# Decoder kernel: decay exponents from running gate sums brought in by DMA, some norm steps on GpSimd, two reorderings on TensorE, and dummy products in the tail

## The reference, cut to what matters

```python
q = l2norm(silu(h @ Wq)); k = l2norm(silu(h @ Wk)); v = silu(h @ Wv)
beta = sigmoid(h @ Wb)
g = -exp(A_log) * softplus(h @ Wa + dt_bias)
alpha = exp(g)
def step(S, (q_t, k_t, v_t, a_t, b_t)):
    S = S * a_t
    delta = (v_t - k_t @ S) * b_t
    S = S + outer(k_t, delta)
    return S, (q_t @ S) * scale
o = rms_norm(scan(step)) * o_norm_w * silu(h @ Wg)
x = x + o @ Wo
m = rms_norm(x)
y = x + square(relu(m @ W_fc)) @ W_proj
x = layernorm(x0 + y)            # then cross attention, layernorm, experts, layernorm
```

## Time and profile before

| | before |
|---|---|
| median of 3 runs | 709.38 us (707.37 to 709.8) |
| profiled execution, its own time | 709.69 us |
| its span, first to last instruction | 707.7 us |
| busy in the span: PE / DVE / ACT / POOL | 614.6 / 476.1 / 407.2 / 276.4 us |
| weight loads on PE | 507.6 us |
| mean granted clock of TensorE | 0.917 |

### The profile page before, as it was taken

One profiled execution on the slowest core, in us unless ns is written; L12 is line 12 of the kernel. 1 busy time (PEld: TensorE's weight loads), 2 busy tenths in 40 slices (PEclk: granted clock), 3 DMA queues, 4 the chain that ended last, 5 costly groups with the idle time before them and its releaser, 6 DMA issues.

```text
span 707.7 us, 14886 instructions
## 1 busy us (share of the span) xinstructions
PE 614.6 (87%) x5453; PEld 507.6 (72%) x5453; DVE 476.1 (67%) x1841; ACT 407.2 (58%) x723; POOL 276.4 (39%) x233
## 2 busy tenths in 40 slices
PE   2889999999998999999988999999899986339940
PEld 1456887888888778888787888887888875227740
DVE  4747944787888568888895787679657864513315
ACT  2734537898755587876646878756154653114413
POOL 3446002444444125426421443474212252226763
PEclk9999969999998999999999999999589997559985
DMA  8403130002105100020050002001401430032243
GB/s 253 154 1 75 46 70 1 2 1 46 31 1 115 17 1 15 2 49 24 21 128 3 1 16 46 16 20 48 81 1 44 161 87 10 13 72 27 24 93 107
DMA packets 78383, 34.02 MB, mean 48 GB/s; under 512 B 49968, under 2 KB 73849, under 8 KB 78184
## 3 DMA queue, kind: packets, MB, share of 16 engines
q1 hardware_dynamic: 74344, 30.89, 17.2%
q0 software_dynamic: 3968, 2.20, 2.3%
HBM read 20.04 MB, written 14.40 MB: 49 GB/s over the span
## 4 chain that ended last, share of the span: by engine, by line
PE 63%; DVE 18%; issue 6%; ACT 5%; DMA 4%; POOL 3%; SPq 1%; ACTq 0%; POOLq 0%; DVEq 0%
PE ps L681 21%; PE ps L646 6%; PE ps L722 4%; DVE prod L1868 4%; DVE blk_t L1875 4%; PE ps L834 3%; PE ps L1255 3%; PE ps L745 3%; PE ps L1245 3%; PE ps L822 3%; PE ps L1051 2%; PE ps L920 2%; PE ps L930 1%; POOL slots L595 1%; PE ps L941 1%
## 5 line engine op out<-in xcount | busy, mean ns | idle before, releaser
L490 POOL TENSOR_TENSOR att<-att,br 128x512 f32<-128x512 f32 x32 | 33.3, 1043 | 179.1 <-ACT att L1318 179.1
L471 POOL TENSOR_TENSOR of<-oss,mhalf 128x4 f32<-128x4 f32 x32 | 32.7, 1021 | 86.8 <-DVE oss L1762 86.2
L471 POOL TENSOR_TENSOR st<-st,mhalf 128x4 f32<-128x4 f32 (+1 forms) x23 | 22.4, 973 | 100.8 <-DVE st L1988 67.1
L1868 DVE TENSOR_TENSOR prod<-kn,blk_t 128x126 f32<-128x126 f32 (+35 forms) x244 | 53.0, 256 | 1.1 <-DMA kn<-n_blocks 1.1
L1875 DVE TENSOR_TENSOR blk_t<-blk_t,prod 128x126 f32<-128x126 f32 (+35 forms) x244 | 51.3, 249 | 0.1
L1264 ACT ACTIVATE uo<-ps 128x512 f32<-128x512 f32 x56 | 33.6, 600 | 20.0 <-PE ps L681 19.8
L1264 ACT ACTIVATE ogT<-ps 128x512 f32<-128x512 f32 x32 | 19.1, 596 | 42.9 <-PE ps L646 42.7
L681 PEld LDWEIGHTS ps<-kT 128*128 128x128 f32 x256 | 32.7, 192 | 14.9 <-issue 14.5
L681 PE MATMUL ps<-qT,kT 128*128 128x128 f32 x256 | 42.9, 324 | 0.4 <-DVE att L1767 0.4
L941 PEld LDWEIGHTS ps<-ones,kT 128*128 128x128 f32 x256 | 32.6, 192 | 11.5 <-issue 10.7
L1725 DVE SCALAR_TENSOR_TENSOR uo<-uo,of,gate_sb 128x128 f32<-128x128 f32 x128 | 38.6, 363 | 3.1 <-POOL of L471 3.1
(11 more groups left out here) (249 smaller groups left out, 1764.6 us busy)
## 6 DMA issues: line engine op xcount, KB each, us to landing
tt_blocks<-gate_sb SPq DMA_DIRECT2D x4, 512.0 KB, 3.0
TT<-tt_blocks SPq DMA_DIRECT2D x16, 128.0 KB, 2.6
Nm<-in_L_ffn_w SPq DMA_DIRECT2D x1, 2048.0 KB, 9.1
kn<-in_L_ffn_w SPq DMA_DIRECT2D x8, 256.0 KB, 4.5
n_blocks<-Nm SPq DMA_DIRECT2D x16, 96.0 KB, 2.6
kn<-n_blocks SPq DMA_DIRECT2D x4, 384.0 KB, 3.4
t_blocks<-blk_t SPq DMA_DIRECT2D x4, 384.0 KB, 2.3
slots<-qT SPq DMA_DIRECT2D x5, 274.0 KB, 3.9
```

The costliest lines, as they stand in the source:

```text
L471: pool.tensor_tensor(out_ap, in_ap, mhalf[:, 0:n], ALU.pow).then_inc(done, 1)
L490: pool.tensor_tensor(heads(att[:, slot(kb, m)]), heads(att[:, slot(kb, m)]), bc(br[:, kb % 2, unit(m)].unsqueeze(2), [P, HG, P]), ALU.mult ...
L1868: counts.append(st.step(tt(pr, bc(bn_[:, j, i0:i0 + n].unsqueeze(2), [P, n, ncol]), bc(blk_t[:, j, 0:ncol].unsqueeze(1), [P, n, ncol]), AL ...
```

## The change

Decay. `head_eg` now splits g into a part on a coarse grid and a rest, and beside the three sums of before it makes a fourth and one product that gives the running sums as 32 rows of 128. ACT copies the negated sums as columns (`neg_sums`) and the rows (`sum_rows`). SP stores the rows to memory and loads them back, spread over all partitions, one load of 128 by 512 for each unit (two large ones of 128 by 2048 for batch 0). POOL adds the -30000 above the diagonal (`decay_mask`), and ACT takes exp with the column as bias, one instruction for each of the four heads (for batch 0 DVE subtracts the column and masks in `first_exponents`, and ACT takes exp in one instruction). PE's `decay` is gone. `head_eg` is moved into the middle of `between`, ahead of `q_proj` 4, and `v_proj` 4 waits until ACT has read the bank.

Banks. The key projections of batches 1 to 3 go to `EB` in place of `KS`, and the key grams of batch 0 alternate between two banks.

GpSimd. The scaling of the rows of h (`head_h`), two norm steps of four instructions each (`post_a`, `post_x2`) and the clearing of `blk_t` go from DVE to POOL. The final half-products keep theirs on DVE.

Order. `gate_out` stands ahead of the post pieces on DVE. `qk_gram` 3 and 4 stand ahead of `post_y`. `post_aT` stands after the transpose of the first key unit in `levels`. ACT makes its last copy of level 4 before the next silu.

Dummy products. `keep_busy(n)` issues n products of 128 by 512 in bf16 whose result nobody reads, at eight places of the tail and 32 ahead of the experts.

```diff
-            def decay_cols(kb, m):
-                pool.wait_ge(sm["gate_step"], kb * GATE_OPS + GATE_G)
...
+            def decay_mask(kb, m):
+                pool.wait_ge(*decay_loaded(kb, m))
+                a = heads(att[:, slot(kb, m)])
+                pool.tensor_tensor(a, a, bc(masked.unsqueeze(1), [P, HG, P]), ALU.add).then_inc(sm["gm_ok"], 1)
...
+            def store_sums(kb):
+                sp.wait_ge(sm["eg_ok"], 2 * kb + 1)
+                sp.dma_start(decay_rows(kb), sum_rows[:]).then_inc(sm["sums_stored"], 16)
+                sp.wait_ge(sm["sums_stored"], (kb + 1) * 16)
+
+            def load_sums(kb, m, n=1):
+                if kb >= 1 and m >= 2:
+                    sp.wait_ge(*after("au_ps", kb - 1, NU, m - 2))
+                    sp.wait_ge(*after("gm_ok", kb, NU, m - 2))
...
+            store_sums(0)
+            for m in (0, NU // 2):
+                load_sums(0, m, NU // 2)
             for b in range(B):
+                kb = b + 1
                 exchange_n(b)
+                if kb < B:
+                    store_sums(kb)
...
-            def decay(kb, m):
-                pe.wait_ge(*after("gm_ok", kb, NU, m))
...
-                mm(bank[:], ident_h[:], bc(neg_h[:, :].unsqueeze(1), [P, HG, P]), start=True, stop=False, skip_group_check=True)
-                mm(bank[:], gt, att[:, slot(kb, m)], start=False, stop=True, skip_group_check=True).then_inc(sm["e_ps"], 1)
...
+                    if n == EG_AT and kb + 1 < B:
+                        pe.wait_ge(sm["eg_ok"], 2 * (kb + 2))
...
                 if old:
                     out_proj(b, NU - 1)
+                if nxt:
+                    head_eg(kb + 1)
                 q_proj(kb, 4)
...
-                if nxt:
-                    head_eg(kb + 1)
                 q_sums(kb, 7)
+                for n in range(3, 5):
+                    qk_gram(kb, n)
                 if old:
                     post_y(b)
-                for n in range(3, 5):
-                    qk_gram(kb, n)
...
+            def keep_busy(n):
+                for _ in range(n):
+                    mm(ps[KS][:], ident_h[:], bc(ident_h[:, :].unsqueeze(1), [P, HG, P]), start=True, stop=True)
...
             def decay_exp(kb, m):
-                act.wait_ge(*after("e_ps", kb, NU, m))
-                A(att[:, slot(kb, m)], ps[e_bank(kb, m)][:], ACT.Exp).then_inc(sm["dt_exp"], 1)
+                act.wait_ge(*after("gm_ok", kb, NU, m))
...
+                for h in range(HG):
+                    a = att[:, slot(kb, m), hs(h)]
+                    last = A(a, a, ACT.Exp, bias=neg_sums[:, m * HG + h:m * HG + h + 1])
+                last.then_inc(sm["dt_exp"], 1)
...
                 l3_copy(b, 2)
                 l4_copy(b, 1)
+                l4_copy(b, 3)
                 if key:
                     k_silu(kb, 1)
-                l4_copy(b, 3)
-                if key:
                     k_square(kb, 1)
```

More of the change, by code:

```diff
@@ L430, in _ @@
                 exchange_t(b)
+                if kb < B:
+                    for m in range(5):
+                        load_sums(kb, m)
                 if b >= 1:
@@ L433, in _ @@
                     store_x2(b - 1)
+                if kb < B:
+                    for m in range(5, NU):
+                        load_sums(kb, m)
             sp.wait_ge(*after("l3_ps", B - 1, 4, 3))
@@ L508, in step @@
                     decay_beta(kb, m - 1)
-                if kb < B and m < NU:
-                    decay_cols(kb, m)
+                if b >= 1 and s == 2:
+                    post_x2(b - 1)
+                if kb + 1 < B and s == 3:
+                    head_h(kb + 1)
                 if b == B - 1 and s == 5:
@@ L518, in step @@
                     out_power(b, s)
+                if kb < B and m < NU:
+                    decay_mask(kb, m)
                 if 1 <= b < B - 1 and s == NU - 1:
@@ L605, in _ @@
             pool.memset(TT[:], 0.0).then_inc(sm["fills_ok"], 1)
-            for m in range(NU):
-                decay_cols(0, m)
             for m in range(NU):
@@ L707, in head_eg, with sums_of @@
                 else:
[L708 to L712 removed]
+                    pe.wait_ge(*after("v_ok", b - 1, NU, EG_AT - 1))
+                high, low = g_all[:, 0], g_all[:, 1]
+                bank = ps[EB]
+                def sums_of(i, tri, g, start=True, stop=True):
+                    return mm(bank[:, i * NP:(i + 1) * NP], tri, g, start=start, stop=stop, skip_group_check=True)
+                sums_of(0, le, high)
+                sums_of(1, ones[:], high, stop=False)
+                sums_of(1, ones[:], low, start=False)
+                sums_of(2, gt, high, stop=False)
+                sums_of(2, ones[:], low, start=False)
+                sums_of(3, le, low)
+                mm(bank[0:NP, 2 * P:3 * P], high, le, start=True, stop=True, skip_group_check=True).then_inc(sm["eg_ps"], 1)
             def k_proj(kb, m):
@@ L1204, in _ @@
             k_transpose(0, NU - 1)
-            head_eg(0)
-            decay(0, 0)
-            decay(0, 1)
             for m in range(NU):
@@ L1786, in step @@
                     rhs(b, s + 1)
+                if scan and s >= 1 and not last_key:
+                    gate_out(b, s - 1)
                 if kb >= B and s == 5:
@@ L1791, in step @@
                     post_piece(b, s)
-                if nxt and s == 3:
-                    head_ss(kb + 1)
-                if scan and s >= 1 and not last_key:
-                    gate_out(b, s - 1)
                 if nxt and s == NU - 1:
@@ L1821, in step @@
                         post_choice(b - 1)
-                    if s == 2:
-                        post_x2(b - 1)
-                if nxt and s == 3:
-                    head_h(kb + 1)
                 if nxt and last_key:
@@ L1828, in step @@
                         gate_op(kb + 1, i)
-                if key and s == 4:
-                    clear(kb)
             def post_piece(b, s):
@@ L1925, in between @@
                 eliminate(kb, aside)
-                for n in range(3):
+                for n in range(5):
                     att_mult(kb, n)
@@ L2147, in _ @@
                     setup_b()
+                if m >= 5:
+                    first_exponents(m - 5)
+            for m in range(3, NU):
+                first_exponents(m)
             end_factors()
```

223 lines of the change are left out of this document (143 added, 80 removed).

## The result

| | before | changed |
|---|---|---|
| median of 20 runs | 708.66 us (701.65 to 713.41) | 703.48 us (700.14 to 711.41) |
| ratio to before | | 0.9944 (95%: 0.9916 to 0.9972) |
| the same, beside the later runs (control) | 709.01 us | 699.85 us, 0.9882 (0.9848 to 0.9916) |
| profiled execution | 709.69 us, span 707.7 | 709.15 us, span 707.1 (control 697.99, span 696.0) |
| mean granted clock in it | 0.917 | 0.940 (control 0.956) |

The change gains 4 to 8 us by the two ratios, not the 24.5 of the forecast, and the time lies outside the range that was given (the control's median, 699.85, inside it). One kernel's executions differ by several microseconds: those of the changed kernel run from 700.14 us (clock 0.948) to 711.41 (0.928).

The account below looks back on a forecast made before the run. PE was taken to bound the scans, with ACT 1.49 us per step behind. Terms -16.8 - 3.6 + 1.4 + 0.5 - 1 - 5 = -24.5 took 709.7 to 685 us; range for 8 in 10 674 to 702.

Parts of the forecast that it names:

- What bounds the scan: Scans: PE bounds the step of 9.91 us; after the change ACT is the longer engine, at 8.97.
- A: Scan steps preparing units 1 to 7 of three batches: 21 x 0.8 = 16.8 us less, bounds 9.4 and 22.7.
- B: levels for batches 0 to 2: 1.2 us less each, 3.6 in all, bounds 0 and 3 x 1.5.
- the third rival: POOL in the scans: GpSimd is starved, four norm instructions at 3.3 us each, slower at 741 us; chance 0.07.
- C: between: +2.2 for the first, 0.8 less for each of two, +0.8 for the third; in sum +1.4 us.
- D: Setup: last key product at 56 to 60 us, taken as +0.5 us, bounds -1.5 and +3.
- E: Scan of batch 3: the norm leaving DVE and the earlier gate_out give -1 us, between 0 and -2.
- F: Tail and experts: dummies holding the upper clock level give -5 us in sum, bounds -7 and +1.
- the first: Rival, scans: ACT becomes the bound at the dear exp price, step 9.46 us, total 697 us; chance 0.18.
- The second: Rival, scans and clock: PE keeps its full gain and the clock stays up, 674.5 us; chance 0.11.
- The fourth: Rival, scans: loads of the sums land later than a step, PE waits where decay stood, 708 us; chance 0.05.

Follow-up runs that it names:

- run 4: Changed kernel with norms on DVE, post_y ahead of the query-key products and no dummies, leaving the running sums and small edits: ratio to before 1.0125.
- run 15: The running sums alone measured once more (norms on DVE, post_y first, no dummies): ratio to before 1.013.
- run 10: Changed kernel with only h's power and scaling put behind the output's power and the mask on POOL: 697.19 us, ratio to before 0.9847.
- run 8: Kernel before the change with the dummy products alone added, at the same places: ratio to before 0.9893.
- run 9: Changed kernel without its running sums, the decay made as before, all else as changed: ratio to before 1.006.
- run 1: Changed kernel with the two norm steps and the scaling of h back on DVE from POOL: ratio to before 1.0085.
- run 7: Running sums alone (norms on DVE, post_y first, no dummies) with one exp for four: one execution, scans 63.2, 69.3 and 67.6 us, no ratio.
- run 12: Changed kernel without the running sums, with h's power and scaling behind the output's power on POOL: ratio to before 1.002.

## Why the prediction was wrong

- **What bounds the scan** was right for the step read: ACT's step there is 9.00 us, where 8.97 was forecast. For the scan it was not. **The step that failed is A: 21 x 0.8.** The price per step was measured on one step and multiplied by 21. That step lost 1.06, more than the 0.8. But the steps differ in PE's work, and where PE has least (1 and 6), it now waits for ACT: they got longer. A came out at 4.6 us in the control, 7.8 with the norms on DVE (runs 4 and 15), under the lower bound of 9.4, and 9.6 in run 10, just over it. Of each, about 3 us are clock and not the sums. That is an estimate from step 0 of the kernel before: in scans 0 and 1 it took 8.42 and 9.37 us, at 0.81 and 0.82 of the clock; at 1.00 it took 6.87 (scan 0 of run 8) and 7.74 (scan 2).
- **The small edits of order** were costed at nothing, or at a gain in B. Of the 1.1 us that steps 0 and 1 of scan 2 lose in the control, run 9 loses 0.8 without the running sums.
- **The norm steps on POOL** were costed at nothing. They cost the scans 3 us (207.9 against 204.6 in run 1), and the third rival names the place, the output's power behind the scaling of h (not the decay's factors: those stand ahead of it, at 155.76). Only its price was far too high (0.60 to 0.80, not 3.3). Run 10 takes it out.
- **C** has the second error: -0.8 for each of two. Batch 1 came out so (-0.7). But `level1` came 8.95 us after the send in batch 0 (+4.2, and by PE's own work, not by ACT's copy as was argued) and 2.7 and 3.4 later in batches 2 and 3, since `post_y` now starts after the elimination. I had seen the bound (+1) and took the other side. With the 2.7 us between the scans' ends and the sends, C is about +12, not +1.4.
- **What was not in the sum** is that these orders go with a higher clock: `levels` 1 to 3 went from 68.4 to 55.2 us in the control, at 1.00 instead of 0.92, 0.92 and 0.57 (to 61.6 in the first profile, at 1.00, 0.92 and 0.91). Forecast B: 2.4. Gain and loss of `between` and levels nearly cancel.
- **D** (+0.5) was small, but within its bounds: the last key product came 2.0 us later, and the blocks 0.8. **E** was wrong by a little, +0.2 for -1. **F** was right in cause and size: -4.6 and -4.9 for -5; run 8 shows that the dummies alone make it. Its parts held in the first profile (-2.1 up to the first expert, -2.9 in it); in the control, whose first expert is still at 4.11, they were -4.0 and -1.2.
- **The rivals**: the first holds for some steps (run 7), at 1.28 us per four exps rather than 1.63. The second is refuted. The fourth is not what happened, since the loads land in 3.3 us, but its outcome, near no change, is close to the measured one.
- **Sum**: A, B and C were forecast at -19.0 and came to about -8 in the control, to about +1 in the other profile. That the levels made good much of what C cost is luck: no term said so.

The parts don't add. The dummies alone give 0.989; the sums with the small edits cost 1.3%; norms and orders with the dummies, without the sums, are at 1.006 (run 9); all of it at 0.988. What the sums are worth depends on the rest: they shorten the scans by 7.8 us against the kernel before (run 4) and by 13.0 between runs 12 and 10 (215.9 to 202.8, 2.1 of it the wait that the edit adds). What is shown is where pieces of that come from: norms on DVE block the levels' copies once `post_y` is late (run 1), and h's scaling holds up the output's power (run 10). Why the clock in the levels holds in one order and not in the other was not isolated. The six profiles with `post_y` first, and run 1's, have 68.0 us or more in `levels` 1 to 3; the ten with `post_y` late and the norms on POOL have 55.0 to 63.9. But no run changed the waits there and nothing else.

## What to carry to other kernels

Before multiplying a gain by the number of steps, read two or three different steps, above all those where the bounding engine has least to do: the second engine bounds there first. Compare steps only where the granted clock is the same. On an in-order queue, put work with a late deadline behind what the bounding engine waits for in the same step; moving five instructions (run 10) took 5.0 us off the scans, as much as the whole change had (4.6). And test the cheapest part alone: the dummies, 77 products, were as fast as the whole change.

## What was not expected of the hardware

- VectorE slows beside GpSimd outside the elimination too: the four scaled products of a gated output, with two inputs in SBUF (the on-chip memory), took 2.92 us at 160.18, while POOL worked on 128x512 tiles, and 1.13 in the step before. This agrees with the Trainium skill, "GPSIMD Engine Reference", "1. Specifications", on shared ways into SBUF, seen from DVE's side.
- One kernel's time goes with its granted clock from execution to execution, loosely: over the 20 executions of the changed kernel the correlation is -0.85 (700.47 us at 0.955, 711.41 at 0.928, but 702.37 at 0.942 and 710.02 at 0.943). Which of the two drives the other isn't shown.
- In setup the granted clock fell to its lower level while PE idled for 8.38 us, and stayed there when it went on (windows of the changed kernel: the idle, and PE at work after it):

```profile
36.00:47.40 11.40, 2.35 (x19) 1.93 (x18) 11.33 (x39) 5.77 (x10) 2.11 (x2) 0.78 0.01 2
47.40:56.00 8.60, 7.67 (x33) 7.13 (x34) 5.67 (x16) 0.71 (x2) 5.01 (x5) 0.50 0.00 0
```
